# Gated linear attention and a five-matrix feed-forward block: the end of the last token block rewritten, and new call orders

## The reference

```python
q, k, v = x @ Wq, x @ Wk, x @ Wv              # 16 heads of 8 features
g = sigmoid(x @ Wf + bf)                      # forget gate
state = state * g[..., None] + v[..., None] * k[..., None, :]   # 8 x 8 per head, over the tokens
out = einsum('bhij,bhj->bhi', state, q)
out = layernorm(out) * gamma + beta           # over the 128 features
x = layernorm(x + (out * silu(x @ Wg)) @ Wout)
h = silu(x @ w1.T * s1) * (x @ w2.T * s2)     # 512 wide, ternary weights
h = gelu(h @ h1.T * sh1)                      # 512 x 512
h = gelu(h @ h2.T * sh2)                      # 512 x 512
x = layernorm(x + h @ w3.T * s3)              # back to 128
```

## Time and profile before

| | us |
|---|---|
| median of three runs | 511.95 |
| profiled execution | 511.54 |
| its span, first to last instruction | 509.6 |
| TensorE busy | 496.3 |
| VectorE busy | 448.7 |
| ScalarE busy | 406.4 |
| GpSimd busy | 311.7 |

### The profile page before, as it was taken

One profiled execution on the slowest core, in us unless ns is written; L12 is line 12 of the kernel. 1 busy time (PEld: TensorE's weight loads), 2 busy tenths in 40 slices (PEclk: granted clock), 3 DMA queues, 4 the chain that ended last, 5 costly groups with the idle time before them and its releaser, 6 DMA issues.

```text
span 509.6 us, 7946 instructions
## 1 busy us (share of the span) xinstructions
PE 496.3 (97%) x2528; PEld 382.4 (75%) x2528; DVE 448.7 (88%) x708; ACT 406.4 (80%) x839; POOL 311.7 (61%) x363
## 2 busy tenths in 40 slices
PE   8999999999999999999999999999999999999995
PEld 5576777777878777786877777786877777787995
DVE  4999989999999899998999999899999999993352
ACT  5775968888887888978797788988778987868863
POOL 0751848668392766848385765938477683929432
PEclk9999999999999999999999999999999999999998
DMA  6899999953994497689969675799719483710001
GB/s 244 205 267 236 255 263 241 230 125 84 275 221 104 104 246 177 154 195 249 259 183 234 142 185 125 186 222 244 196 51 235 130 194 94 183 25 1 23 23 44
DMA packets 21500, 87.33 MB, mean 171 GB/s; under 512 B 2512, under 2 KB 3280, under 8 KB 13520
## 3 DMA queue, kind: packets, MB, share of 16 engines
q1 hardware_dynamic: 21168, 86.46, 67.9%
q10 hardware_dynamic: 288, 0.33, 0.2%
HBM read 74.72 MB, written 12.06 MB: 170 GB/s over the span
## 4 chain that ended last, share of the span: by engine, by line
PE 48%; POOL 17%; DVE 13%; issue 13%; ACT 7%; DMA 1%; POOLq 0%; DVEq 0%; ACTq 0%
PE F L2342 26%; POOL h1lo L479 5%; PE front L2243 5%; POOL h2lo L479 5%; PE back L2441 4%; DVE KJ L1590 3%; DVE QJ L1597 2%; POOL KJ L541 2%; DVE QJ L1605 2%; PE ps_v L2243 2%; PE back L2328 2%; PE back L2227 1%; DMA out<-res 1%; POOL rstd_o L511 1%; POOL y L553 1%
## 5 line engine op out<-in xcount | busy, mean ns | idle before, releaser
L903 ACT ACTIVATE h<-F,cols 128x512 f32<-128x512 f32 x120 | 80.7, 686 | 17.0 <-PE F L2342 16.5
L479 POOL TENSOR_TENSOR h1lo<-h,h1hi 128x512 fp32r<-128x512 f32 x60 | 76.5, 1291 | 12.8 <-ACT h1hi L896 12.7
L547 POOL TENSOR_TENSOR QJ<-QJ 128x512 f32<-128x512 f32 x14 | 18.0, 1284 | 108.0 <-DVE QJ L1605 108.0
L479 POOL TENSOR_TENSOR h2lo<-h,h2hi 128x512 fp32r<-128x512 f32 x60 | 77.2, 1309 | 4.9 <-ACT h2hi L896 4.7
L1590 DVE TENSOR_TENSOR_SCAN KJ<-g,carry,KJ 128x512 f32<-128x512 f32 x64 | 78.5, 1263 | 0.9 <-ACT carry L829 0.8
L1590 DVE TENSOR_TENSOR_SCAN KJ<-g,KJ 128x512 f32<-128x512 f32 x64 | 74.3, 1202 | 1.6 <-POOL KJ L528 0.7
L1597 DVE TENSOR_TENSOR QJ<-QJ,KJ 128x1024 f32<-128x1024 f32 x60 | 72.9, 1237 | 0.2
L2342 PE MATMUL F<-h2hi,whi 128*128 128x512 f32 (+1 forms) x256 | 71.6, 415 | 0.8 <-ACT h L903 0.7
L2342 PE MATMUL F<-h1hi,whi 128*128 128x512 f32 (+1 forms) x256 | 68.9, 410 | 1.6 <-DVE h L1654 1.3
L2342 PE MATMUL F<-h1lo,whi 128*128 128x512 f32 (+1 forms) x256 | 67.4, 400 | 0.2 <-POOL h1lo L479 0.2
L2342 PE MATMUL F<-h2lo,whi 128*128 128x512 f32 (+1 forms) x256 | 65.7, 397 | 0.0
(11 more groups left out here) (184 smaller groups left out, 935.9 us busy)
## 6 DMA issues: line engine op xcount, KB each, us to landing
KJ<-qk_bounce SPq DMA_DIRECT2D x30, 1024.0 KB, 9.9
QJ<-qk_bounce SPq DMA_DIRECT2D x30, 1024.0 KB, 11.0
qk_bounce<-qk SPq DMA_DIRECT2D x30, 256.0 KB, 4.6
x_in<-in_x SPq DMA_DIRECT2D x16, 256.0 KB, 11.4
xT<-in_xT SPq DMA_DIRECT2D x15, 256.0 KB, 11.5
out<-res SPq DMA_DIRECT2D x15, 256.0 KB, 3.3
wraw<-in_wffn SPq DMA_DIRECT2D x2, 1024.0 KB, 6.6
wraw<-in_wffn SPq DMA_DIRECT2D x2, 256.0 KB, 4.6
```

Of the source, the lines that this page charges most:

```text
L479: e.tensor_tensor(h_lo[layer][:, t, :w], h[:, t, :w], h_hi[layer][:, t, :w].bitcast(f32), ALU.subtract).then_inc(lo_done[layer], 1)
L547: e.tensor_tensor(first, first, other, ALU.add).then_inc(add_gp_done, 1)
L903: e.activation(dst[:, t, :WIDTH[n]], F[t][:, :WIDTH[n]], ACT.Gelu, scale=scale[t]).then_inc(gelu_done[layer], 1)
```

## The change

It has two parts.

First, the end of the last block. `last_half` becomes `last_half_begin` and `last_half_end`: each chunk has a PSUM bank of its own (`last_bank`), the products of k = 0 to 2 of both chunks are given first and those of k = 3, which need the half's last GELU, last. Each chunk counts up the semaphore, and the residual is added chunk by chunk. Statistics, shift and the norm with mean are gone: the squares are summed (three chunks on VectorE with `scalar_tensor_tensor` and its sum, the third chunk on ScalarE in `square_third`), and the result is only scaled; of half 1, one chunk on ScalarE and one on VectorE (`norm_last`). In TensorE's list half 0's third layer stands in the middle of half 1's second middle layer. `norm_2(14)` and `save_carry(15)` stand behind the last GELU in ScalarE's list.

Second, the lists of all engines are ordered anew: which loads SyncE issues first, where a projection, a transpose or a norm stands among the feed-forward calls, and in what order the first block prepares weights and low parts. Every list has the same calls as before but for the rewritten end. `rest` is shown here for its last part, ScalarE's list for its first and last parts, SyncE's and GpSimd's for a few lines.

```diff
@@ -198,6 +198,9 @@
 
         def half_bank(half, t):
             return (F, (ps_v, g, front, back))[half][t]
+
+        def last_bank(c):
+            return c // NL + 2 * (c % NL)
 
...
@@ -299,7 +302,7 @@
 
             def store_half(h):
                 n, t = NB - 1, half_tokens(h)
-                e.wait_ge(norm_half_done[h], 1)
+                e.wait_ge(norm_half_done[h], 1 + h)
                 e.dma_start(out_d[:, AT[n] + t.start:AT[n] + t.stop], res[n % 2][:, t]).then_inc(stored[n % 2], 16)
 
...
@@ -318,150 +321,150 @@
                 e.dma_start(w3_scale[:], w3s_d.broadcast_to([P, D])).then_inc(w3_landed, 16)
 
             load_projections(0)
-            load_projections(1)
-            load_cols()
-            load_xT(1)
             load_weights(0)
             load_weights(1)
+            load_cols()
+            load_projections(1)
+            load_xT(1)
             load_weights(2)
-            load_xT(2)
             send(1, 1)
             load_w3()
+            load_xT(2)
...
@@ -514,10 +517,10 @@
 
             def rstd_half(h):
                 n, cs = NB - 1, slice(ENDS[h].start, ENDS[h].stop)
-                r, sh = rstd["2"][:, n % 2, cs], shift["2"][:, n % 2, cs]
-                e.wait_ge(mv_half_done[h], 1)
+                r = rstd["2"][:, n % 2, cs]
+                e.wait_ge(squared_half[h], 2)
                 e.wait_ge(norm_done["2"], n - 1)
-                e.tensor_tensor(r, mv["2"][:, cs, 1], eps4[:, cs], ALU.add).then_inc(ve_half_done[h], 1)
+                e.tensor_tensor(r, square2[:, cs], eps4[:, cs], ALU.add).then_inc(ve_half_done[h], 1)
                 e.wait_ge(ve_half_done[h], 1)
                 e.tensor_tensor(r, r, mhalf4[:, cs], ALU.pow).then_inc(pow_half_done[h], 1)
...
@@ -944,14 +947,20 @@
                     last = e.activation(w3[:, k, :], w3[:, k, :], ACT.Identity, bias=w3_mean[:, k:k + 1])
                 last.then_inc(w3_centered, 1)
 
-            def norm_half():
+            def square_third():
+                n, c = NB - 1, ENDS[1][0]
+                e.wait_ge(r2_half_done[1], 1)
+                e.wait_ge(ve_done["2"], n)
+                e.activation(x1[n % 2][:, chunk(c)], res[n % 2][:, chunk(c)], ACT.Square, scale=D ** -0.5,
+                             accum_out=square2[:, c:c + 1]).then_inc(squared_half[1], 1)
+
+            def norm_half(h):
 
                 n = NB - 1
-                e.wait_ge(shift_half_done[0], 1)
-                for c in ENDS[0]:
-                    last = e.activation(res[n % 2][:, chunk(c)], res[n % 2][:, chunk(c)], ACT.Identity,
-                                        bias=shift["2"][:, n % 2, c:c + 1], scale=rstd["2"][:, n % 2, c:c + 1])
-                last.then_inc(norm_half_done[0], 1)
+                e.wait_ge(pow_half_done[h], 1)
+                for c in ENDS[h][:2 - h]:
+                    last = e.activation(res[n % 2][:, chunk(c)], res[n % 2][:, chunk(c)], ACT.Copy, scale=rstd["2"][:, n % 2, c:c + 1])
+                last.then_inc(norm_half_done[h], 1)
 
             def hi_0(which):
...
             tanh(0)
-            copy_v(0)
+            split_weights(0)
+            hi_0(1)
             g_of_tanh(0)
-            hi_0(1)
-            sum_low_parts(0)
             copy_k(1)
+            split_weights(1)
             copy_qj(0)
             copy_kj(2)
             copy_qj(1)
             copy_kj(4)
-            split_weights(0)
             copy_qj(2)
             tanh(1)
+            sum_low_parts(0)
             copy_qj(3)
             sum_low_parts(1)
             copy_k(2)
             copy_kj(6)
-            sum_low_parts(2)
             silu_gate(0)
             copy_v(1)
-            split_weights(1)
+            g_of_tanh(1)
+            copy_q(1)
             save_carry(0)
-            copy_q(1)
-            g_of_tanh(1)
+            center_w3()
             tanh(2)
             silu_gate(1)
             norm_o(0)
-            tanh(3)
+            sum_low_parts(2)
             affine(0)
             sum_low_parts(3)
             split_weights(2)
+            tanh(3)
             split_weights(3)
             silu_gate(2)
             norm_1(0)
             copy_k(3)
             x1_hi(0)
+            silu(0, 0)
...
@@ -1496,46 +1506,47 @@
             gelu(1, 14, 1)
             hi(2, 14, 1)
             gelu(1, 14, 2)
+            gelu(1, 14, 3)
             hi(2, 14, 2)
-            gelu(1, 14, 3)
             hi(2, 14, 3)
-            norm_2(12)
             square(13)
             norm_1(15)
             gelu(2, 14, 0)
-            save_carry(15)
+            gelu(2, 14, 1)
             x1_hi(15)
-            gelu(2, 14, 1)
             gelu(2, 14, 2)
             gelu(2, 14, 3)
             tail_silu(0, 0)
             tail_silu(0, 1)
             tail_silu(1, 0)
+            tail_silu(0, 2)
             tail_silu(1, 1)
-            tail_silu(0, 2)
             tail_silu(0, 3)
             tail_silu(1, 2)
             tail_silu(1, 3)
             tail_gelu(1, 0, 0)
             tail_gelu(1, 0, 1)
             tail_gelu(1, 0, 2)
-            norm_2(13)
             tail_gelu(1, 0, 3)
             tail_gelu(1, 1, 0)
             tail_gelu(1, 1, 1)
             tail_gelu(1, 1, 2)
             tail_gelu(1, 1, 3)
             square(14)
+            norm_2(13)
             tail_gelu(2, 0, 0)
-            norm_2(14)
-            tail_gelu(2, 1, 0)
             tail_gelu(2, 0, 1)
             tail_gelu(2, 0, 2)
             tail_gelu(2, 0, 3)
+            tail_gelu(2, 1, 0)
             tail_gelu(2, 1, 1)
             tail_gelu(2, 1, 2)
             tail_gelu(2, 1, 3)
-            norm_half()
+            norm_2(14)
+            save_carry(15)
+            norm_half(0)
+            square_third()
+            norm_half(1)
 
...
@@ -1662,38 +1673,29 @@
                 e.tensor_tensor(res[n % 2][:, :w], back[:, :w], x1[n % 2][:, :w], ALU.add).then_inc(r2_done, 1)
 
             def residual_half(h):
-                n, t = NB - 1, half_tokens(h)
-                e.wait_ge(w3_half_made[h], 1)
-                if h == 0:
-                    e.wait_ge(stored[n % 2], landed(n - 2))
-                e.tensor_tensor(res[n % 2][:, t], F[h][:, t], x1[n % 2][:, t], ALU.add).then_inc(r2_half_done[h], 1)
-
-            def stats_half(h):
                 n = NB - 1
-                e.wait_ge(r2_half_done[h], 1)
-                for c in ENDS[h]:
-                    last = e.bn_stats(stats["2"][:, c, :], res[n % 2][:, chunk(c)])
-                last.then_inc(stats_half_done[h], 1)
-                e.wait_ge(stats_half_done[h], 1)
-                for c in ENDS[h]:
-                    last = e.bn_aggr(mv["2"][:, c, :], stats["2"][:, c, :])
-                last.then_inc(mv_half_done[h], 1)
-
-            def shift_half(h):
-
-                n, cs = NB - 1, slice(ENDS[h].start, ENDS[h].stop)
-                e.wait_ge(pow_half_done[h], 1)
-                e.wait_ge(mv_half_done[h], 1)
-                e.scalar_tensor_tensor(shift["2"][:, n % 2, cs], mv["2"][:, cs, 0], -1.0, rstd["2"][:, n % 2, cs],
-                                       ALU.mult, ALU.mult).then_inc(shift_half_done[h], 1)
-
-            def norm_second_half():
+                for i, c in enumerate(ENDS[h]):
+                    e.wait_ge(w3_half_made[h], i + 1)
+                    if h == 0 and i == 0:
+                        e.wait_ge(stored[n % 2], landed(n - 2))
+                    e.tensor_tensor(res[n % 2][:, chunk(c)], F[last_bank(c)][:, chunk(c)], x1[n % 2][:, chunk(c)], ALU.add).then_inc(r2_half_done[h], 1)
+
+            def square_half(h):
+
                 n = NB - 1
-                e.wait_ge(shift_half_done[1], 1)
-                for c in ENDS[1]:
-                    last = e.tensor_scalar(res[n % 2][:, chunk(c)], res[n % 2][:, chunk(c)], rstd["2"][:, n % 2, c:c + 1],
-                                           shift["2"][:, n % 2, c:c + 1], ALU.mult, ALU.add)
-                last.then_inc(norm_half_done[1], 1)
+                e.wait_ge(ve_done["2"], n)
+                for i, c in enumerate(ENDS[h]):
+                    if h and i == 0:
+                        continue
+                    e.wait_ge(r2_half_done[h], i + 1)
+                    e.scalar_tensor_tensor(x1[n % 2][:, chunk(c)], res[n % 2][:, chunk(c)], 1.0 / D, res[n % 2][:, chunk(c)],
+                                           ALU.mult, ALU.mult, accum_out=square2[:, c:c + 1]).then_inc(squared_half[h], 1)
+
+            def norm_last():
+                n, c = NB - 1, ENDS[1][-1]
+                e.wait_ge(pow_half_done[1], 1)
+                e.tensor_scalar(res[n % 2][:, chunk(c)], res[n % 2][:, chunk(c)], rstd["2"][:, n % 2, c:c + 1], None,
+                                ALU.mult).then_inc(norm_half_done[1], 1)
 
 
             def tail_hmul(half, t):
...
@@ -1767,8 +1769,8 @@
             scan(1, 6)
             half_norm("1")
             qs(1, 0)
+            set_flag()
             qs(1, 1)
-            set_flag()
             x1_lo(0)
```

(41 more changed lines are left out.)

972 lines of the change are left out of this document (484 added, 488 removed).

## The result

The changed kernel takes 514.62 us (median of 8 runs, 513.18 to 515.51) where the kernel before, run beside it, takes 512.20 (8 runs, 511.70 to 512.82). The ratio is 1.0044, 95% interval 1.0031 to 1.0058: slower by 0.4%, outside the forecast range. The profiled execution of after (515.51 us, span 513.7) is its slowest run and that of before (511.54, 509.6) a quick one, so the two traces differ by 4.1 us and the medians by 2.4.

What follows compares the result with a forecast made beforehand. TensorE was taken to bound the middle, about 28.5 of 28.99 us per block. Terms -0.5 (end), -0.5 (block 14), +0.2 (tail), +0.8 (first block) sum to 0.0: forecast 511.9 us, range 509.4 to 513.8.

Steps and rivals of the forecast that it cites:

- The end, -0.5: Last block: last scaling ends at 506.9 instead of 507.43, so -0.5 us, between -0.9 and 0.
- Giving them last hides nothing that shows: Last block: TensorE doesn't wait for half 1's last GELU, now or before, so putting its dependent products last gains nothing visible.
- The two stores before it are out by then: End of kernel: the two earlier stores are finished when the last scaling ends at 506.9; no size given.
- The tail of TensorE, +0.2: TensorE's last products: low products of half 1 wait for a GpSimd low part; +0.2 us, between nothing and 0.74.
- The first block, +0.8: Start to first feed-forward product: ScalarE's moved work delays norm_1(0), partly absorbed later; +0.8 us, between 0 and +2.0.
- The rival with 2.1 us: First block: low parts of weight piece 2 delay norm_1(0), all 2.1 us reach the first feed-forward product; 513.5, chance 0.26.
- the low sum: First block, ScalarE: reading and summing weight piece 2's low parts, moved between norm_o(0) and affine(0), costs 2.1 us there.
- The rival's bound: First block: the slower case decides once norm_1(0) starts later than about 41.5; at 39.39 it costs nothing.
- set_flag takes nothing off since norm_1(0) comes last: First block, VectorE: giving the flag for TensorE's branch one qs earlier gains nothing, as norm_1(0) is later.
- The middle, 0 for the rest and -0.5 in block 14: Middle blocks: one GELU wait in block 14 goes, -0.5 us; all other reordered calls taken as 0.
- the bounds of -3 and +2: Middle blocks: ends of the range, in us, for all reordered calls other than block 14's, which were taken as 0.
- The halving: VectorE's sum over squares, last block: two float32 SBUF sources halve throughput, 0.42 instead of 0.35 us; end's best case -0.8.

Runs made afterwards that it cites:

- orders-alone run: The change's new call orders up to the first product of block 15, with the old kernel's end functions and tail order; 514.48 us, ratio 1.0049.
- the end alone: The old kernel's lists up to the last block, the change's functions and lists from there; 512.96 us beside 512.50, ratio 1.0012.
- the end mended: The changed kernel with norm_2(14) back between block 15's GELUs and block 14's store back ahead of both half stores; 516.09 us, ratio 1.0073.
- the gate's projection early: The changed kernel with SyncE's head as before and block 2's gate projection ahead of the 16 filler calls; first product at 46.97, no kernel time given.
- blocks 1 to 7 as before: The changed kernel with the old order for blocks 1 to 7 on all five engines; 514.66 us, ratio 1.0056.
- one product of GpSimd: The changed kernel with kv_gp(7, 6) moved back behind lo(1, 5, 3), where the old kernel has it; 514.59 us, ratio 1.0052.
- SyncE's whole list: New orders on four engines, with the old kernel's end and SyncE's whole list as before; 539.07 us.

## Why the prediction was wrong

Three terms of the sum failed: the end was to gain 0.5 us and loses 0.6 in the trace, the middle was put at nothing and costs 1.4 to 1.7, and the first block was put at 0.8 and costs 1.2 to 1.9 in all profiles but one. The cause of the first is shown, that of the last in part, and that of the middle, the largest, stays open.

- **The end, -0.5.** The computing was right in its parts and better in sum: norm_2(14) behind the last GELU, ScalarE's square releasing GpSimd, -0.8 from TensorE's end to the last scaling. What failed is that the store behind it was taken to cost what it costs in before, 2.2 us from its issue to the end of the span; it takes 3.6. It meets TensorE's fetch of instructions behind its jump. Two things moved towards each other: the store 0.8 earlier, and the jump about 1 us later, because TensorE comes to its last four products only after a GELU that ends at -1.0 instead of -2.5. "Giving them last hides nothing that shows" was true of the products and false of the jump. "The two stores before it are out by then" was false too (the 256-KB store is issued at 508.74, 2.1 us before it lands, and the last store at 510.14), but with the same stores in front and no jump the last row is out 1.35 us behind the issue.
- **The tail of TensorE, +0.2.** Measured 0.22, and that is luck: I had it wait for a low part from GpSimd, and no wait of TensorE of 0.04 us or more is shown there. At two places, neighbouring products stand 0.20 us apart instead of 0.12.
- **The first block, +0.8.** Measured +1.2 to +1.9 in the trace (five of six profiles; +0.7 in one). The rival with 2.1 us had the right size and the wrong cause, and so had the forecast: the low sum sets nothing. What the runs show is SyncE's new order of loads, which brings block 1's K fetch and block 1's input later (0 to 1.5 us), and a slow start of TensorE in some profiles (0.9). I had given the loads 0.4 and never followed block 1's. The rival's bound was off as well: the first product follows norm_1(0) by 3.1 us, so norm_1(0) costs from about 40.9 on, not from 41.5 (at 41.31 the product came at 44.43). And "set_flag takes nothing off since norm_1(0) comes last" was wrong: in before's order the flag comes last.
- **The middle, 0 for the rest and -0.5 in block 14.** Measured +1.4 to +1.7 for blocks 1 to 13, inside the bounds of -3 and +2, on the side to which I gave little. Putting it at nothing had no reason but the two bounds. Block 14 gained 0.1 at most: the wait of the earlier trace rows went, and the orders-alone run needs 50.80 us from block 13's third layer to the last product, before 50.84. The largest new wait is named, and removing it gained 0.27 of its 0.90 us; about half of the loss is idle time of TensorE, the rest stands in its busy time, and I have not shown where it comes from.
- **The sum** of the trace is +4.1, with the first product of a late profile. By medians it is +2.4, the end alone has +0.5 and the orders alone +2.0. By the ratios it is 2.3, 0.6 and 2.5. The intervals are 0.5 to 0.7 us wide to each side, so the two parts add up as far as the runs can tell.
- **VectorE's square** took 0.29 us for 128 columns with two float32 sources (both the same tile), as the single-source scaling at 509.71 does (0.29), and 0.08 for its sum. The halving that the Trainium skill states (Vector Engine (DVE) Microarchitecture Reference, "Points that are easy to get wrong") isn't seen here; by it I had 0.42.

## What to carry to other kernels

At the end of a kernel, ask of the last store not only when it is issued but what its DMA engines do then; an issue 0.9 us earlier gave 0.3 in one profile and lost 0.5 in another. Where orders move, follow the loads of the first block through SyncE's list and ask which engine's queue stands behind each landing, before the engine that looks fullest. Ask too which signal a branch waits for: here it was a flag, and not the long chain beside it. Before a difference of 1 us at a kernel's start is put down to an order, take more than one profile. Lists of calls that were arranged together are hard to mend or mix call by call: five of the changes tried here (the end mended, the gate's projection early, blocks 1 to 7 as before, one product of GpSimd, SyncE's whole list) made a new wait.

## What the hardware showed beside this

- With a jump at TensorE's end, two 16-KB instruction packets come, the second 2.1 to 2.2 us behind the end of the first (2.4 in one profile); the second takes 0.9 to 1.7 us, and a store's share on that DMA engine waits for its end.
- The jump over the other branch ahead of the first product costs 5.3 us, and 1.3 more through the granted clock, which is 0.50 from 46.00 to 52.80.
- TensorE's first projection runs at half pace in some profiles, its products 0.85 us apart instead of 0.43, and VectorE's first product comes up to 0.9 us later by it.
- The same order of calls reached `rstd_o` between 29.55 and 30.92 in different profiles, while the 410 us behind the first product repeat within 0.25.
